# Attention with heads in pairs on halves of TensorE's rows, V's products in pieces in every slot, and other PSUM banks

## What is computed

```
q, k, v = split_heads(x @ Wq), split_heads(x @ Wk), split_heads(x @ Wv)
attn = softmax(einsum('bhqd,bhkd->bhqk', q, k) * 256 ** -0.5)
out  = einsum('bhqk,bhkd->bhqd', attn + bias, v)
x    = layernorm(x + affine_norm(out))
```

## Time and profile before

| | us |
|---|---|
| median of 3 runs | 2537.9 (2537.69 to 2538.2) |
| the profiled execution | 2538.21 |
| its span, first to last instruction | 2536.4 |
| `attention`, first to last instruction in the span | 1035.0 to 1634.1 |
| join behind it | 1644.1 to 1748.2 |
| `route` and `experts` of the last layer | 1749 to 2476 |

### The profile page before, as it was taken

How to read it: one execution, slowest core, us unless ns; L and a number is a source line. 1 busy time by engine, 2 the same in 40 slices (tenths; PEclk the granted TensorE clock), 3 DMA queues, 4 the chain that set the end, 5 groups by cost and what they waited for, 6 DMA issues and landing times. The chain is left out here.

```text
span 2536.4 us, 28877 instructions
## 1 busy us (share of the span) xinstructions
PE 1997.4 (79%) x7612; PEld 1140.5 (45%) x7613; DVE 1398.2 (55%) x2430; ACT 906.8 (36%) x1443; POOL 746.9 (29%) x609
## 2 busy tenths in 40 slices
PE   4778876533996598599999999724469999999990
PEld 2333332523664354234444444224346666666660
DVE  6777775755112522566767667387944444444445
ACT  4665555400332231155555555411013333333330
POOL 3444332011442002100000000022026666666653
PEclk8888888655998699699999999855789999999995
DMA  3000000640112775434434344145433433433318
GB/s 104 0 0 1 0 17 33 202 149 10 60 56 81 274 249 198 80 54 63 68 57 69 53 65 59 36 137 190 129 125 61 66 63 62 65 60 63 62 22 265
DMA packets 161530, 215.90 MB, mean 85 GB/s; under 512 B 27219, under 2 KB 116702, under 8 KB 161120
## 3 DMA queue, kind: packets, MB, share of 16 engines
q1 hardware_dynamic: 119840, 141.75, 21.8%
q0 software_dynamic: 41600, 73.07, 13.0%
HBM read 136.90 MB, written 83.23 MB: 87 GB/s over the span
## 5 line engine op out<-in xcount | busy, mean ns | idle before, releaser
L1736 DVE TENSOR_REDUCE att_MX<-att_s_ps 128x1 f32<-128x512 f32 x512 | 349.2, 689 | 162.4 <-PE att_s_ps L1620 161.6
L1720 ACT ACTIVATE att_PT<-att_st_ps 128x1024 f32<-128x1024 f32 x256 | 262.0, 1023 | 259.9 <-PE att_st_ps L1642 259.8
L1175 PE MATMUL f_h_ps<-W,f_XT 128*128 x736 | 352.0, 601 | 1.1 <-issue 0.6
L1142 POOL DMA_INDIRECT moe<-f_Y,TOK x184 | 270.0, 1468 | 272.0 <-ACT f_Y L1246 256.5
L1190 PE MATMUL f_y_ps<-W,f_HT 128*128 x1472 | 348.3, 379 | 1.7 <-DVE f_HT L1279 1.7
L300 PE MATMUL rec_gate<-rec_XC,rec_W 128*128 128x512 f32 x384 | 200.2, 682 | 102.5 <-ACT rec_R L223 81.5
L1190 PEld LDWEIGHTS f_y_ps<-W,f_HT 128*128 128x128 f32 x1472 | 265.5, 190 | 31.6 <-issue 3.1
L1656 PE MATMUL att_o_ps<-att_PT,V 128*17 128x512 f32 x1024 | 265.2, 598 | 0.1
L1620 PE MATMUL att_s_ps<-att_K,att_Q 128*128 128x512 f32 x512 | 239.8, 474 | 29.2 <-DMA att_Q<-att_Q 25.7
L1620 PEld LDWEIGHTS att_s_ps<-att_K,att_Q 128*128 128x128 f32 x512 | 98.6, 193 | 252.7 <-DVE att_MX L1736 191.8
L1279 DVE COPY f_HT<-f_ht_ps 128x512 f32<-128x512 f32 x184 | 125.9, 684 | 150.6 <-PE f_ht_ps L1183 148.2
(11 more groups left out here) (210 smaller groups left out, 2776.2 us busy)
## 6 DMA issues: line engine op xcount, KB each, us to landing
W<-in_w POOLq DMA_DIRECT2D x48, 512.0 KB, 11.7
x<-n_Y SPq DMA_DIRECT2D x24, 512.0 KB, 4.2
n_X<-x SPq DMA_DIRECT2D x24, 512.0 KB, 8.7
n_Y<-moe SPq DMA_DIRECT2D x24, 512.0 KB, 8.8
att_Q<-qk_pairs SPq DMA_DIRECT2D x96, 128.0 KB
att_K<-qk_pairs SPq DMA_DIRECT2D x96, 128.0 KB
qk_pairs<-prj_HI SPq DMA_DIRECT2D x16, 512.0 KB, 3.3
qk_pairs<-prj_LO SPq DMA_DIRECT2D x16, 512.0 KB, 5.4
```

The lines of the kernel that those rows point to most:

```text
L1142: nc.gpsimd.indirect_dma_start(out=outs[n % len(outs)], out_offset=bass.IndirectOffsetOnAxis(ap=TOK[:, n:n + 1], axis=0), in_=Y[n % R][:], ...
L1175: mm = nc.tensor.matmul(h_ps[r % 2][:], XT[r % 2][:, c], W1[:, bass.ds(e * W_EXPERT + c * F, F)], start=(c == 0), stop=(c == DC - 1))
L1720: nc.scalar.activation(PT[i % 4][:, 2 * half:2 * half + 2].rearrange("p k s -> p (k s)"), st_ps[half][:], ACT.Exp, scale=SCALE).then_inc(s ...
L1736: nc.vector.tensor_reduce(MX[n % 2][:, qc, h:h + 1], s_ps[m % 2][:], AX.X, ALU.max).then_inc(s_mx, 1)
```

## The change

Inside `attention`:
- Stacks hold two pairs of heads per group: `i` runs over 64 pairs (head p and head p + 2 of a group), one on rows 0 to 49, the other on rows 64 to 113. A product reads 48 rows (scores) or 50 (transposed scores) of one half. There are 4 stacks instead of 3, twelve loads per group instead of seven, and only rows 32 to 63 and 96 to 127 are preset.
- Scores: the two `s_ps` banks belong to the halves, one each. LEAD is 4 pairs, two groups.
- Transposed scores: `st_ps` is two tiles of two banks as before, a bank for each half; the exponential takes both halves of one block of keys, and two `PT` tiles hold a group each, four heads wide.
- V's products: 8 pieces per group (block of keys by half of the queries, 256 columns), each for all four heads, one group behind, one piece in nearly every slot.
- VectorE splits the maxima into high and low parts before they are transposed (8 columns instead of 4), so ScalarE alone copies them; VectorE's last addition moves to GpSimd; the copy of V's sums and the transposes run one group later.

Outside: the loads of `W1` move from `relative_part` to the join behind attention, where GpSimd issues them first.

```diff
-def join(nc, tag, x, ys, out, ident, *, ..., bufs=GROUPS):
+def join(nc, tag, x, ys, out, ident, *, ..., bufs=GROUPS, background=()):
...
+            for dst, src, loaded in background:
+                pool.dma_start(dst, src).then_inc(loaded, 16)
             st.clear_old(pool)
...
-STACKS = 3
+STACKS = 4
-LEAD = HG + 2
+TWO = HEADS // 2
+LEAD = 4
+HALF = P // 2
...
-        PT = [st.sb(f"PT{k}", [P, KC, S]) for k in range(4)]
+        PT = [st.sb(f"PT{k}", [P, HG, KC, S]) for k in range(2)]
-        st_ps = [st.ps(f"st_ps{k}", (P, 2 * BANK)) for k in range(2)]
+        st_ps = [st.ps(f"st_ps{k}", (P, 2, BANK)) for k in range(2)]
...
+            for half in range(2):
+                for i, (pq, pk) in enumerate(((0, 0), (1, 0), (0, 1))):
+                    at = half * HALF + i * DH
+                    eng.dma_start(Q[k][at:at + DH].bitcast(F32), rows(0, pq, half)).then_inc(s_ld[k], 16)
+                    eng.dma_start(K[k][at:at + DH].bitcast(F32), rows(1, pk, half)).then_inc(s_ld[k], 16)
...
+            for n in range(NGROUPS + 3):
+                if n < NGROUPS:
+                    stack_maxima(n)
+                if n >= 3:
+                    add(n - 3)
...
+            def scores(i, qc, half):
+                if half == 1 and p == 0 and qc == 0:
+                    pe.wait_ge(s_ld[k], LOADS * (n // STACKS + 1))
+                if m >= 1:
+                    pe.wait_ge(s_mx, 2 * m - half)
+                at = slice(half * HALF, half * HALF + ROW_M)
+                nc.tensor.matmul(s_ps[half][:], Q[k][at, p, qc * P:(qc + 1) * P], K[k][at, p],
+                                 start=True, stop=True).then_inc(s_smm, 1)
...
+            def scores_T(i, kc, half):
+                m = i * KC + kc
+                if half == 0 and m >= 2:
                     pe.wait_ge(s_p, m - 1)
+                at = slice(half * HALF, half * HALF + ROW_M + 2)
+                mm = nc.tensor.matmul(st_ps[m % 2][:, half], K[k][at, p, kc * P:(kc + 1) * P], Q[k][at, p],
+                                      start=True, stop=True)
...
+            def sums(n, piece):
+                kc, q = piece // 2, slice(piece % 2 * (S // 2), (piece % 2 + 1) * (S // 2))
+                if piece == 0:
+                    pe.wait_ge(s_p, 2 * KC * (n + 1))
+                    if n >= 1:
                         pe.wait_ge(s_ot, n)
+                for h in range(HG):
+                    mm = nc.tensor.matmul(o_ps[32 * h:32 * h + VW, q], V[:, b * KC + kc, g * HG + h], PT[n % 2][:, h, kc, q],
+                                          start=(piece == 0), stop=(piece == PIECES - 1))
...
+            for i in range(TWO):
+                n, p = i // 2, i % 2
+                for slot in range(KC):
+                    at = KC * p + slot
+                    scores_T(i, slot, 0)
+                    if i + LEAD < TWO:
+                        scores(i + LEAD, slot, 1)
+                    if at >= 1 and n >= 1:
+                        sums(n - 1, at - 1)
+                    if i + LEAD < TWO:
+                        scores(i + LEAD, slot, 0)
+                    scores_T(i, slot, 1)
+                    if at == PIECES - 1 and n >= 1:
+                        sums(n - 1, at)
+                    if p == 0 and slot == 1 and n + 1 < NGROUPS:
                         maxima(n + 1)
+                    if p == 0 and slot == 3 and n >= 2:
+                        sums_T(n - 2)
...
+                if p == 0 and n >= 2:
+                    act.wait_ge(s_pv, n - 1)
+                for kc in range(KC):
+                    act.wait_ge(s_stm, m + 1)
+                    nc.scalar.activation(PT[n % 2][:].rearrange("p (a b) k s -> p a b k s", b=2)[:, :, p, kc], st_ps[m % 2][:],
                                          ACT.Exp, scale=SCALE).then_inc(s_p, 1)
+                    if p == 0 and kc == 0 and n >= 2:
+                        copy_sums(n - 2)
+                    if p == 0 and kc == 1 and n + 1 < NGROUPS:
+                        copy_maxima(n + 1)
...
+                for half in (1, 0):
+                    dve.wait_ge(s_smm, 2 * m + 2 - half)
+                    nc.vector.tensor_reduce(MX[n % 2][:, qc, half, p:p + 1], s_ps[half][:], AX.X, ALU.max).then_inc(s_mx, 1)
...
+            def split(n):
+                own.after(nc.vector.tensor_copy(MS[n % 2][:, :, :, 0], MX[n % 2][:]))
+                nc.vector.tensor_tensor(MS[n % 2][:, :, :, 1], MX[n % 2][:], MS[n % 2][:, :, :, 0].bitcast(F32),
+                                        ALU.subtract).then_inc(s_ms, 1)
...
-            relative_part(nc, rel, V, ident, att_rel, expert_loads(W1, None, w1_1, w2_1, E1, s_w1))
+            relative_part(nc, rel, V, ident, att_rel)
...
-                 bufs=GROUPS // 2)
+                 bufs=GROUPS // 2, background=expert_loads(W1, None, w1_1, w2_1, E1, s_w1))
```

More of the change, by code:

```diff
@@ L415, with join @@
 T_LAG = 3
-def join(nc, tag, x, ys, out, ident, *, yT=None, rms_w=None, affine=None, outT=None, router=None, logits=None, bufs=GROUPS):
+def join(nc, tag, x, ys, out, ident, *, yT=None, rms_w=None, affine=None, outT=None, router=None, logits=None, bufs=GROUPS,
+         background=()):
     N = bufs
@@ L1546, in attention @@
         block = ctx.enter_context(nc.Block())
-        LOADS = 7 * 16
+        LOADS = 12 * 16
+        PER = H // HG
+        PIECES = 2 * KC
         def where(n):
-            return n // (H // HG), n % (H // HG)
+            return n // PER, n % PER
         def load(eng, n):
@@ L1555, in load, with rows @@
             if n >= STACKS:
[L1556 to L1563, removed]
+                eng.wait_ge(s_stm, 2 * KC * (n - STACKS + 1))
+            def rows(m, part, half):
+                c0 = (g * HG + 2 * half) * DH
+                return qk[m, part, c0:c0 + 2 * DH, b * S:(b + 1) * S].rearrange("(h d) s -> d h s", d=DH)
+            for half in range(2):
[3 more added lines that the diff above has]
+                    eng.dma_start(K[k][at:at + DH].bitcast(F32), rows(1, pk, half)).then_inc(s_ld[k], 16)
         def tokens(a, b):
@@ L1569, in _ @@
         def _(sp):
[L1570 to L1579, removed]
+            for n in range(NGROUPS):
+                if n < STACKS:
+                    sp.wait_ge(s_set[n], 2)
+                load(sp, n)
+                b, g = where(n)
+                if g == 2:
+                    if b >= 2:
+                        sp.wait_ge(s_st[b % 2], 16 * (b // 2))
+                    sp.dma_start(OUT[b % 2][:], tokens(rel_out, b)).then_inc(s_rel[b % 2], 16)
@@ L1596, in _ @@
-            for n in range(NGROUPS):
-                k = n % STACKS
-                for row, (tile, ready) in enumerate(((MH, s_mh), (ML, s_ml))):
-                    pool.wait_ge(ready, n + 1)
-                    pool.dma_start(Q[k][ROW_M + row:ROW_M + row + 1].bitcast(F32), tile[n % 2][:].bitcast(F32)).then_inc(s_mr[k], 16)
-                b, g = where(n)
-                if b >= 1 and g == 1:
-                    store(b - 1)
-            store(B - 1)
+            for k in range(2, STACKS):
+                for half in range(2):
+                    at = half * HALF + 32
+                    nc.gpsimd.memset(K[k][at:at + 32].bitcast(F32), -1.0).then_inc(s_set[k], 1)
@@ new lines, in stack_maxima, with add @@
+            def stack_maxima(n):
+                k = n % STACKS
+                pool.wait_ge(s_mh, n + 1)
+                for half in range(2):
+                    at = half * HALF + ROW_M
+                    pool.dma_start(Q[k][at:at + 2].bitcast(F32), MH[n % 2][half * HG:(half + 1) * HG].bitcast(F32)).then_inc(s_mr[k], 16)
+            def add(n):
+                b, g = where(n)
+                pool.wait_ge(s_tmp, n + 1)
+                if g == 0:
+                    pool.wait_ge(s_rel[b % 2], 16 * (b // 2 + 1))
+                o = OUT[b % 2][:, :, g * HG * DH:(g + 1) * HG * DH]
+                nc.gpsimd.tensor_tensor(o, o, TMP[n % 2][:].rearrange("p k h d -> p k (h d)"), ALU.add).then_inc(s_o, 1)
+                if g == PER - 1:
+                    pool.wait_ge(s_o, n + 1)
+                    pool.dma_start(tokens(out, b), OUT[b % 2][:]).then_inc(s_st[b % 2], 16)
@@ L1639, in scores_T @@
                     pe.wait_ge(s_p, m - 1)
[L1640 to L1651, removed]
-                        pe.wait_ge(s_ot, n)
[L1653 to L1658, removed]
+                at = slice(half * HALF, half * HALF + ROW_M + 2)
@@ L1675, in _ @@
                 for qc in range(KC):
[L1676 to L1689, removed]
-                        maxima(n + 1)
[L1691 to L1694, removed]
+                    for half in (1, 0):
+                        scores(i, qc, half)
+                    if i == 2 and qc == 1:
+                        maxima(0)
+            for i in range(TWO):
+                n, p = i // 2, i % 2
+                for slot in range(KC):
[11 more added lines that the diff above has]
+                    if p == 0 and slot == 1 and n + 1 < NGROUPS:
```

(13 more changed lines are left out.)

157 lines of the change are left out of this document (62 added, 95 removed).

## The result

| | before | changed | 
|---|---|---|
| median of 4 runs, us | 2537.8 (2537.4 to 2538.2) | 2645.5 (2642.7 to 2648.5) |
| ratio | | 1.0425, interval 1.0407 to 1.0443 |
| span of the profiled execution | 2536.4 | 2640.7 |
| attention | 599.1 | 688.8 (1034.2 to 1723.0) |
| join behind it | 104.1 | 118.9 (1733.1 to 1852.0) |

The two stages hold the whole loss: 89.7 and 14.8 us, against 104.3 for the span. The page of the changed kernel, sections 1 and 2; in the second line each digit is the granted clock of TensorE in a fortieth of the span, in tenths of full speed.

What follows compares the result with a forecast made beforehand. TensorE was taken to bound attention, 17.65 us a group; VectorE and ScalarE would take over at 15.0. Profiled execution 2538.2 less 79.6 in attention plus 5 in the join gave 2464 us, range 2405 to 2530.

Steps and rivals of the forecast that it cites:

- The rival's price: Attention: TensorE often stands still and its clock falls to half; group near 22.7 us, total 2690 us; chance 6%.
- the stand: TensorE's wait before each group's first sums piece, for ScalarE's copy of earlier sums; 1.6 us a group, covered by nothing.
- the slots: Main loop's new unit, 8 a group, two score, two transposed products and a sums piece; 1.40 us each, 11.2 a group.
- VectorE's work: Between reduces in each group: reciprocal and scaling 0.70 us, splitting the maxima 0.50; together 1.2.
- the join: Stage behind attention: the 16 moved expert-weight loads delay its additions and input; +5 us, bounds 0 and 12.
- the loop over the exponentials: Main loop: transposed scores' two buffers wait for the exponential two slots back; 2.80 us for two slots, 1.40 each.
- Borders to full-row transposes: Entering and leaving row tiling at two places in each group; 0.2 us, within 1.05 for the transposes.
- halves one after the other: Rival, main loop: row halves do not overlap; slot 1.67 us, group 16.35, total 2503 us; chance 14%.
- two and two column groups: Rival, V's sums: only two of four column groups run at once; group 16.9 us, total 2519, up to 2535; chance 10%.
- neither overlap: Rival, main loop: no halves or column groups overlap; slot 2.11 us, group 19.4, total 2594 us, slower; chance 10%.
- The rival in which the waits hide each other: Main loop: slots at 1.30 us, half the copy's wait covered; group 13.0, total 2406 us; chance 12%.
- The signs named beforehand: Mid-attention: TensorE below 95%, VectorE 80% or more, groups 15 us, gap 1.3 to 1.6, pair and record starts, later join reduce.

Runs made afterwards that it cites:

- copy first: Changed kernel with ScalarE's copy of V's sums moved ahead of the first exponential of a group; 2426.2 us, 0.956 of the kernel before.
- filled-stand run: Changed kernel, order untouched, with slot 1's first transposed product issued six times more where TensorE waits for the copy; 2460.0 us.
- thin-product run of the old kernel: Kernel before, with scores reading rows 0 to 47 and transposed scores rows 0 to 49 instead of all 128; 2611.6 us.
- the wider weights: Changed kernel with V's products 32 columns of weights wide instead of 17; 2633.7 us.
- pair of runs with full rows: All score and transposed score products reading 128 rows: in the changed kernel 2494.0 us, with ScalarE's copy also moved first 2463.0 us.

## Why the prediction was wrong

- **The step that failed is the clock.** The sum held TensorE at 1.00 through the main loop. A fall was named as a rival and given 6%, on the ground that in routing TensorE stood still a good part of the time and kept 1.00. Those products read 128 rows. The row was taken for all products, and the runs show that it does not carry over to the changed kernel's: with 128 rows the clock survived a stand even a little longer (15.81 us groups, 1.00), with 48 to 50 rows it didn't. The prediction compared times of being busy and did not ask how many rows the products read. The rival's price was near: 22.7 us a group and 2690 forecast, 21.32 and 2645 measured.
- **It takes two parts of the change together.** Thin products without the stand (copy first): clock kept. The stand with full products: kept. The stand filled with products: kept. Both: 0.55. The stand was in the sum as 1.6 us of waiting that nothing covers; what it does to the clock was not, and neither part was looked at with the other.
- **The rest of the sum held in total, in part by luck.** With the clock up, the filled-stand run gives 2460 us against 2464 forecast, and its groups 14.49 against 15.0. Four terms of the group are off, two each way: the slots took 10.24 instead of 11.2, the stand 1.16 (with the six products) instead of 1.6; the transposes 1.39 instead of 1.05 and VectorE's work 1.7 instead of 1.2. (The last two are read in the copy-first run, from how much later than 1.28 the next pair starts where they stand.) Outside the group, the join took 10 more than forecast and the attention 13 less.
- **The slot** is 1.28 instead of 1.40. The sum for TensorE, 1.30, was right, and the loop over the exponentials, put at 1.40, does not hold it up: TensorE goes through the slot without a gap, 0.34 from pair to pair, 0.38 to the sums, 0.56 for the piece (0.53 forecast). The pairs start under 0.01 apart instead of the 0.11 taken. The bound from the earlier trace rows was right for them, but the step from one pair to the next takes 0.34 where the sum had 0.12. The page TensorE: Matmul & The Clock Gate of the Trainium skill, Part 3, has some 4 ns between tiles in different row groups. These starts, 3 to 7 ns apart, agree.
- **The stand** costs 0.77 us at full clock, not 1.6. The prediction let T1 of the group's first slot start 1.3 after T0, a full slot's pace. But that slot has no sums piece: T0 stands at 1139.36 and T1 at 1139.70, 0.34 later, so the exponential and the copy behind it are over about 1 us earlier than forecast.
- **Borders to full-row transposes** were put at 0.1 a visit; the thin-product run of the old kernel shows 0.32. The TensorEngine Tiling page of the Trainium skill ("Key Properties") names the drain at a change of tiling mode without a price; 0.32 is one from this case.
- **The rivals** of halves one after the other, of two and two column groups, and of neither overlap are all refuted by the starts in the trace. The rival in which the waits hide each other, 13.0 us a group and 2406 us, is what the copy-first run comes near to: 13.33 and 2426, of which the join has 15. Its slot of 1.30 was right, but the wait there is not hidden, it is gone.
- **The join** lost 14.8 us, not 5, over the upper bound of 12. VectorE's first operation came 4.6 us later after the first issue, as forecast. What was not costed is the second group's input, which landed 23.3 us after its issue instead of 8.8.
- **The signs named beforehand:** groups 15 us apart, TensorE under 95% (96%) and VectorE at 80% (54%) fail, as does the length of the gap, 0.71 idle at full clock and 0.55 at half instead of 1.3 to 1.6. The copy as its releaser, the pairs and the four records are all there.

What stays open: why the clock rose in the changed kernel in some groups and not in others, for 225 us not once; what the number of columns does; and whether a shorter stand would be harmless with thin products. None of these was tried apart from the wider weights. In the changed kernel thin products also run side by side, and with full rows they do not, so the pair of runs with full rows changes both at once. Only the old kernel's run with thin products keeps the two apart: nothing runs side by side there, and the rise was late too. For the fall at the stand no run does. Nor does any run tell whether it is the count of rows or the running on a part of the array as such. Most of these runs are single ones; the differences in time on which the account rests are 74 to 219 us.

## What to carry to other kernels

A rearrangement that makes TensorE's work denser in time can put it on fewer rows, and then a short wait can cost far more than its length: here 0.77 us of waiting in each group, some 23 us in all, made a difference of 219. Look first for who waits for whom in the new order, and move that one instruction. Read the clock line of the page before any group of instructions; if products have doubled in length, all else is secondary. A background load is better placed in a stage that does not itself wait for input at that moment: the same 16 loads cost 14 to 15 us at the head of the join and nothing that can be seen in the routing.

## What the runs showed of the hardware

- TensorE's clock stayed at 0.50 for 118 us in which TensorE was never idle, with score products on 48 to 50 rows; with 128 rows the same order of products had 1.00 from 1074.2 on, 2.7 us after the first T. In the changed kernel's family the clock rose at 1076 to 1078 with 128 rows and at 1097 to 1114 with 48 to 50.
- At full clock and with score products on 48 to 50 rows, 0.71 us of idle TensorE ahead of a group's first sums piece was where the clock fell, seven times out of seven; with 128 rows 0.86 us in every group of 15.81 left it at 1.00.
- Products on rows 0 to 49 and 64 to 113 that write different banks start 0.00 to 0.01 us apart. The next pair follows 0.34 us later, where two full-row products one behind the other take 0.47, at full clock.
- Four float32 products in four column groups run side by side as two did: the piece of 8 records, 256 columns of four heads, takes 0.56 us from its start to the next product, at full clock.
- Going from products on 48 or 50 rows to full-row transposes and back costs about 0.32 us (groups of 18.30 against 17.65, two visits each).
- Beside 16 loads of 512 KB from GpSimd's queue, one input of 512 KB landed 23.3 us after its issue on SP instead of 8.8, and SP's next issues took 6.1 to 6.5 us each instead of 1.3 to 2.2.
